# Two adds of a residual sum re-paired: the second norm's h and x2 each go into the convolution's PSUM bank

## The reference, cut to what matters

```
h = relu(layernorm(x));  x = x + L0(h)            # no edge: L0 gives 0
h = relu(layernorm(x));  x = x + agg*... + h      # layer L1; no edge: x + h
h = relu(layernorm(x))                            # layer L2: two convolutions and a residual
out = relu((h @ W1) * norm + b1)
out = (out @ W2) * norm + b2
x = x + (out + h)                                 # <- the sum that the change touches
h = relu(layernorm(x));  x = x + relu(conv(relu(conv(h))) + h)   # layer L3
```

## Time and profile before

| | |
|---|---|
| time, median of 3 runs | 3132.97 us (3106.86 to 3156.36) |
| span of the profiled execution | 2548.9 us |
| own time of the profiled execution | not listed apart; at the median, 584.1 us would lie outside its span |
| TensorE busy | 1809.8 us, 71% |
| VectorE busy | 1878.0 us, 74% |
| ScalarE busy | 1299.9 us, 51% |
| GpSimd busy | 1856.4 us, 73% |
| granted TensorE clock, mean | 0.874 of full |

### The profile page before, as it was taken

One profiled execution on the slowest core, in us unless ns is written; L12 is line 12 of the kernel. 1 busy time (PEld: TensorE's weight loads), 2 busy tenths in 40 slices (PEclk: granted clock), 3 DMA queues, 4 the chain that ended last, 5 costly groups with the idle time before them and its releaser, 6 DMA issues.

```text
span 2548.9 us, 26059 instructions
## 1 busy us (share of the span) xinstructions
PE 1809.8 (71%) x6414; PEld 875.1 (34%) x6414; DVE 1878.0 (74%) x3056; ACT 1299.9 (51%) x2694; POOL 1856.4 (73%) x1775
## 2 busy tenths in 40 slices
PE   3788877774996488878888887768888888860000
PEld 1433333322453243333444343433444344430000
DVE  7999987646888378987999788887999799960000
ACT  2767666532886264545666555545666566620000
POOL 5777777766777777756777577756777677777776
PEclk9999998886998699979999889889999899975555
DMA  2344433224776254443344356563434354440000
GB/s 65 102 125 127 118 109 84 68 72 130 232 241 220 82 167 134 134 129 105 118 125 126 106 163 194 175 190 111 123 120 126 114 145 130 133 133 23 22 22 20
DMA packets 240170, 309.75 MB, mean 122 GB/s; under 512 B 86875, under 2 KB 102389, under 8 KB 239896
## 3 DMA queue, kind: packets, MB, share of 16 engines
q1 hardware_dynamic: 183576, 281.76, 34.5%
q0 software_dynamic: 56448, 26.34, 5.8%
HBM read 188.24 MB, written 144.91 MB: 131 GB/s over the span
## 4 chain that ended last, share of the span: by engine, by line
POOL 20%; DVE 19%; PE 17%; issue 12%; ACT 6%; DMA 1%; DVEq 0%; SPq 0%; ACTq 0%; POOLq 0%
POOL mn_ring L515 12%; POOL out_dram L1883 8%; PE bank L1185 5%; DVE mn_total L1567 4%; DVE node_h L1391 4%; PE bank L1189 3%; PE bank L1194 3%; PE bank L1928 2%; PE bank L1179 2%; PE bank L1199 2%; DVE node_h L1436 1%; DVE mn_scaled L1583 1%; ACT node_square L1312 1%; ACT node_std L1296 1%; DVE node_x L1415 1%
## 5 line engine op out<-in xcount | busy, mean ns | idle before, releaser
L515 POOL DMA_INDIRECT mn_ring<-slot_rows,addr_i x980 | 1036.8, 1058 | 398.0 <-issue 293.7
L1185 PE MATMUL bank<-node_x,center 128*128 128x512 f32 x492 | 257.5, 638 | 73.0 <-DVE node_h L1391 68.9
L515 POOL DMA_INDIRECT found<-node_table,look_i x196 | 212.1, 1082 | 86.4 <-issue 63.8
L1194 PE MATMUL bank<-node_h,wconv 128*128 128x512 f32 x492 | 266.4, 625 | 0.3 <-DVE mn_sums L1701 0.3
L1189 PE MATMUL bank<-node_square,mean 128*128 128x512 f32 x492 | 259.7, 610 | 2.7 <-ACT node_std L1291 2.0
L515 POOL DMA_INDIRECT xin<-in_x_dram,src_i x196 | 205.5, 1048 | 71.7 <-issue 59.4
L1312 ACT ACTIVATE node_square<-bank 128x512 f32<-128x512 f32 x246 | 145.7, 592 | 216.1 <-PE bank L1185 215.9
L515 POOL DMA_INDIRECT xin<-in_x_dram,dst_i x196 | 206.8, 1055 | 63.5 <-issue 59.5
L1306 ACT ACTIVATE node_act<-bank,bias 128x512 f32<-128x512 f32 x246 | 168.3, 684 | 160.0 <-PE bank L1194 159.7
L1883 POOL DMA_INDIRECT out_dram<-keep,scat_i x196 | 193.0, 985 | 62.4 <-issue 62.4
L1199 PE MATMUL bank<-node_act,wconv 128*128 128x512 f32 x442 | 230.2, 603 | 2.5 <-ACT node_act L1306 2.5
(11 more groups left out here) (334 smaller groups left out, 3821.8 us busy)
## 6 DMA issues: line engine op xcount, KB each, us to landing
mn_ring<-local SPq DMA_DIRECT2D x120, 256.0 KB, 4.4
out_dram<-node_rows SPq DMA_DIRECT2D x98, 256.0 KB
mn_rin<-res SPq DMA_DIRECT2D x96, 256.0 KB, 3.7
local<-node_rows SPq DMA_DIRECT2D x96, 256.0 KB
slot_rows<-keep SPq DMA_DIRECT2D x96, 256.0 KB, 2.0
mn_fcol<-f_rows SPq DMA_DIRECT2D x192, 128.0 KB
res<-mn_x SPq DMA_DIRECT2D x72, 256.0 KB, 2.7
node_x_in<-in_x_dram SPq DMA_DIRECT2D x64, 256.0 KB, 2.9
```

Of the source, the lines that this page charges most:

```text
L515: return eng.indirect_dma_start(out=dest, out_offset=None, in_=table, in_offset=bass.IndirectOffsetOnAxis(ap=index, axis=0), bounds_check= ...
L1185: pe.matmul(bank[i][:, :], C["center"][:, :], src, start=True, stop=True).then_inc(s["centered"][i], 1)
L1194: pe.matmul(bank[5 if i == 2 else 1][:, :], C["wconv"][:, 2 * i - 4, :], nd.h[i][:, u % 2, :], start=True, stop=True) \
```

## The change

The sum of x2 and h in SBUF goes. In its place x2 is added to bank 5 together with the bias, in the bank (one SCALAR_TENSOR_TENSOR), and then h is added as the bank's result is written to x3 (one TENSOR_TENSOR). Both stand where x3 stood, after the wait for `conv2(2)`. The sums come in another order, (conv + bias + x2) + h. The buffer `res` is gone and `x2` has three slots, since it is now read one tick later. The number of instructions is the same on every engine.

```diff
-        self.x_in, self.x2, self.res, self.x3 = sb("x_in", 3), sb("x2", 2), sb("res", 2), sb("x3", 3)
+        self.x_in, self.x2, self.x3 = sb("x_in", 3), sb("x2", 3), sb("x3", 3)
...
-            center(2, nd.x2[:, (t - 1) % 2, :], s["x2"], t - 1)
+            center(2, nd.x2[:, (t - 1) % 3, :], s["x2"], t - 1)
...
-            need(act, s["res"], u - 1)
-            act.activation(nd.x2[:, u % 2, :], bank[0][:, :], ACT.Copy).then_inc(s["x2"], 1)
+            need(act, s["res"], u - 2)
+            act.activation(nd.x2[:, u % 3, :], bank[0][:, :], ACT.Copy).then_inc(s["x2"], 1)
...
         if 0 <= t - 2 < n:
             u = t - 2
-            h = normalise(2, u)
-            v.wait_ge(s["h"][2], u + 1)
-            v.wait_ge(s["x2"], u + 1)
-            v.tensor_tensor(nd.res[:, u % 2, :], nd.x2[:, u % 2, :], h, ALU.add).then_inc(s["res"], 1)
+            normalise(2, u)
         if 0 <= t - 3 < n:
             u = t - 3
             v.wait_ge(s["conv2"][2], u + 1)
+            v.wait_ge(s["x2"], u + 1)
+            v.scalar_tensor_tensor(bank[5][:, :], bank[5][:, :], C["bias"][:, 1:2], nd.x2[:, u % 3, :],
+                                   ALU.add, ALU.add).then_inc(s["res"], 1)
             v.wait_ge(s["res"], u + 1)
+            v.wait_ge(s["h"][2], u + 1)
             need(v, s["centered"][3], u - 2)
-            v.scalar_tensor_tensor(nd.x3[:, u % 3, :], bank[5][:, :], C["bias"][:, 1:2], nd.res[:, u % 2, :],
-                                   ALU.add, ALU.add).then_inc(s["x3"], 1)
+            v.tensor_tensor(nd.x3[:, u % 3, :], bank[5][:, :], nd.h[2][:, u % 2, :], ALU.add).then_inc(s["x3"], 1)
```

More of the change, by code:

```diff
@@ L1391, in normalise @@
         v.scalar_tensor_tensor(h, bank[i][:, :], 0.0, nd.std[:, i - 2, :], ALU.max, ALU.mult).then_inc(s["h"][i], 1)
-        return h
     def head(t):
```

## The result

In the measurement that belongs to the prediction the changed kernel takes 3116.55 us (median of 6, 3077.13 to 3131.16), the kernel before 3131.24 us (median of 6, 3106.86 to 3156.36), a ratio of 0.990 with a 95% interval of 0.986 to 0.994. This ratio leaves out runs more than 1.5% above their own kernel's fastest, among them the changed kernel's two longest of six; over all runs the medians stand at 0.995 and the means (3112.6 and 3132.5) at 0.994, so the gain is nearer to half a per cent. I had forecast 3180 us (3146 to 3214). The change stayed within 2%, but it went the other way and left the range.

What follows compares the result with a forecast made beforehand. The prediction took a ring of waits between VectorE and TensorE as the bound. Its terms 29.8 + 8.8 + 1.4 + 6.7 = 46.7 us, added to the measured 3132.97 us, gave 3180 us, range 3146 to 3214.

Steps and rivals of the forecast that it cites:

- A with its last ticks: Stage A: 17 ticks at 0.52 us, 8.8 us more, and 2 ticks at its end at 0.71, 1.4 us more.
- D: Stage D: the chain rests on the gathers, so nothing changes as long as they stay the longer side.
- F: Stage F: 12 ticks at 0.44 us and 2 at 0.71, 6.7 us more.
- C and E: Stages C and E: 21 ticks each at 0.71 us, 29.8 us more; the tick goes from 11.25 to 11.96 us.
- the two ticks at their ends: Ends of stages B, C, D and E: cost covered by waiting for the next stage's first gathers; without cover 5.7 us.
- Work: VectorE's instructions: 10 ns less per unit for 123 units, 1.2 us, counted as nothing.
- Rival 1: VectorE's new idle time in the ring is slack, so the delay is absorbed: 3133 us, within 8; chance 0.12.
- Rival 2: Stage D's gathers get shorter without L1409's contention, 0.048 us each, 9.4 us at most; 3124 us with slack; chance 0.04.
- Rival 3: TensorE loses its clock as the gap at `center` grows from 0.23 to 0.94 us; over 2% slower; chance 0.12.
- the median is 584.1 us above the span, and I take this as unchanged: Measured median against the profile's span of 2548.9 us: the difference stays, so 46.7 us is added to 3132.97 us.
- The ring: VectorE and TensorE waiting on each other each tick; `conv2(2)`'s end to h3's start grows 0.71 us, to 1.42.
- the case "within 2%": Whole kernel: measured time changes by less than 2% (63 us) either way; chance 0.77.

Runs made afterwards that it cites:

- e1_null: The kernel before, unedited, run against itself: 2544.41 us, ratio 1.0002.
- e4_null: The kernel before, unedited, run against itself once more: ratio 0.9994.
- e1_again: The changed kernel, unedited, measured again against the kernel before: 2592.24 us, ratio 1.0195.
- e4_again: The changed kernel, unedited, measured a third time against the kernel before: ratio 1.0199.
- e1_pos: The changed kernel's buffers, but x2 and h summed in SBUF, behind the wait for `conv2(2)`: 2592.07 us, ratio 1.0202 to the kernel before.
- e2: Both kernels with TensorE made late in every tick: the changed one took 1.8 us more with the lateness behind `conv2(2)`, 93.4 us more with it ahead.
- e5_again: The changed kernel, unedited, measured once more against the kernel before: 3122.21 us, ratio 0.9937.
- e3_bias_early: The kernel before with the bias moved into the SBUF sum ahead of the wait for `conv2(2)`: 3141.34 us, ratio 1.002 to the kernel before.
- e5_bias_early: Repeat of e3_bias_early, the kernel before with the bias in the sum ahead of the wait: ratio 0.9997 to the kernel before.
- e3_one_add: The changed kernel without the add of h, so x3 lacks this term: 3134.06 us, ratio 0.9991 to the kernel before.
- e5_one_add: Repeat of e3_one_add, the changed kernel without the add of h: ratio 1.0001 to the kernel before.
- e1_early: The changed kernel's buffers, but x2 and h summed in SBUF, ahead of the wait for `conv2(2)`: 2546.65 us, ratio 1.0016 to the kernel before.
- e2_behind_b: The kernel before with the node input's four transposes done seven times instead of once per tick, behind `conv2(2)`: 2712.98 us.

## Why the prediction was right in its steps and wrong in its number

**The steps.** Times between the first scans of the stages (for F, to the first scatter), mean of two free profiles each (e1_null and e4_null, e1_again and e4_again), against the terms of the sum:

| | before | changed | difference | forecast |
|---|---|---|---|---|
| A with its last ticks | 273.8 | 285.4 | +11.6 | 8.8 + 1.4 |
| B | 285.3 | 285.9 | +0.6 | 0 |
| C | 290.5 | 308.0 | +17.5 | 14.9 |
| D | 282.4 | 278.2 | -4.3 | 0 |
| E | 289.4 | 308.2 | +18.8 | 14.9 |
| F | 250.3 | 257.7 | +7.4 | 6.7 |

The sum is 51.6 us against 46.7. That it comes so near is in part luck: C and E are 6.5 us above their terms together, and D, at which I had put nothing, gives 4.3 back. C and E include the two ticks at their ends, of which I had said that the next stage's gathers cover them. Counted between the first gathers of the stages instead, C costs 14.7 us and D gives back 1.2, so in C the cover held; E costs 17.1, as much as all its 23 ticks at 0.74, so there it did not. The step was 0.74 per tick, not 0.71, since L1410 takes 756 ns (748 expected), L1415 691 (682 expected), and the pair stands 0.80 us apart.

- *Work:* nothing, as said. VectorE's busy time is 1880.2 us in e1_again against 1878.0. Reading the bank cost no more in these rows: the TENSOR_TENSOR at L1415, which reads it, took 691 ns in e1_again, the one in SBUF (L1409) 692 before.
- *Rival 1* (absorbed) is false in the free measurements: idle time and ticks grew together. In the paused ones the tick without a pause grew as well, and yet the time did not.
- *Rival 2* (shorter gathers) is false in the free measurements. Stage D did get shorter, which I had named as its sign, but not by its gathers: they took 1038 ns on the mean before, 1039 in e1_again, and 1036 in e1_pos, which has the SBUF sum, and the two changed kernels take the same time. In C and E the gathers did get shorter (1074 to 1021 and 1084 to 1033 ns), but in e1_pos as well (1028 and 1033), so L1409's operands aren't the reason, and the time did not follow. The rival's 0.048 us per gather is the difference of two rows (0.99 and 1.038 us); that VectorE's instructions cause it, no run shows.
- *Rival 3* (the clock) is false: the granted clock was 0.877 in e1_again, 0.874 in e1_null, and 1.00 in the steady ticks of C, where the gap at `center` had grown to 0.97 us and its four matmuls took 1.95 us. Four of them took 3.75 us in D, and the clock from 1480 to 1486 us of that profile was 0.50 of full; but that a longer gap at `center` brings such a fall, no run shows, so the chance of 0.12, and its part in the 0.20 for slower, were my estimate. The paused runs show means of 0.80 to 0.82 for both kernels alike.

**The step that failed** is the one on the numbers: "the median is 584.1 us above the span, and I take this as unchanged". Nothing of that size lies around the span: a run's time is its span and 1.8 us in the free measurements, and its span and 1.8 to 12 us in the paused ones. The changed kernel's two paused spans (3115.1 and 3100.2 us) are 523 and 508 us longer than its free ones (2591.7 on the mean), so the time lies inside the executions, most of it as pauses, of a kind that the profile that was read did not have at all. A difference of 584 us between span and time was the warning that profile and runs were of different executions, and I treated it as an additive constant. The ring's 46.7 us, right for a free execution (49.4 measured), were then added to a time in which they don't appear: it fell by 14.7 us. So the case "within 2%" came true, but not in the way forecast, and that is luck. With made pauses of TensorE in the ring, e2 shows that 49 us can be anything from 2 to 93, depending on where the lateness falls; a gain it doesn't show.

**What the pauses do to this change.** Ticks between the starts of x3's first instruction, counted in the timelines of paused profiles; "free" counts the ticks that are at most 0.15 us above the tick without a pause, the other number is the excess over it, as the mean of all ticks (A against 10.37 us for the changed kernel, 9.83 for the others):

| profile | tick of C without a pause | C, 20 ticks: free, excess, sum | A, 16 ticks: free, excess |
|---|---|---|---|
| changed, first | 11.99 | 9, 1.51, 270.1 | 16, 0.00 |
| changed, e5_again | 11.99 | 12, 1.03, 260.4 | 13, 2.05 |
| e3_bias_early | 11.19 | 8, 2.27, 269.2 | 2, 3.88 |
| e5_bias_early | 11.19 | 5, 2.12, 266.1 | 4, 4.32 |
| e3_one_add | 11.25 | 8, 2.43, 273.6 | 4, 3.16 |
| e5_one_add | 11.25 | 7, 1.96, 264.2 | 1, 2.38 |

The kernels with the short tick lose more to pauses per tick, those with the long one less, and the sums of 20 ticks overlap. In C the 0.74 us that the ring adds are met by a smaller excess. It is not VectorE's work that decides: e3_one_add has the least of it and the short tick, and is paused like e3_bias_early. Two profiles against four, each of one execution, bear this out as a pattern; they don't prove it. The two profiles of the same changed kernel differ by 33 us over 16 ticks of A, more than the gain; no paused profile of the kernel before exists, so e3_bias_early stands in for it; and no paused run varied the place alone (the kernel of e1_pos, which would, ran only in free measurements). Why a longer tick is paused less, and why enough less to end about 0.5% ahead, if that holds, stays open.

So does the origin of the pauses. Some facts narrow it. They fill idle time in the phases ahead of the node program too, which the change leaves alone (the first scan of stage A starts at 825.4 us in the first profile after, at 602.4 in e1_again), and not in the last, in which GpSimd scatters alone (264.2 and 264.6 us). Transfers don't take longer: the page's share of the queue q1, 28.3% of 3115.1 and 33.8% of 2593.8 us, comes to 882 and 877 us. And the paused traces lack records, 22,492 updates of semaphores in e5_again against 56,542 in e1_null. Every run on record has a recorded span, so whether the recording that loses these records also makes the pauses was not tested.

## What to carry to other kernels

An instruction's place against the wait that closes a ring can count for more than its length: in this kernel the same add (e1_early, e1_pos) leaves the tick of C at 11.25 us ahead of the wait and costs its full spacing, 0.73 us per tick, behind it. Before summing, check that the profiled execution's time is the time that was measured; if they differ by more than the spread of the runs, the sum holds for the profile alone, and the range must take in the executions that it doesn't show. The same change cost 2% in two free measurements and seemed to gain about 0.5% in two paused ones, so a change of 1 to 2% wants more than one measurement, each with a check of which kind it is.

## What the runs showed of the hardware that was not expected

- The same program took 2542 to 2544 us in three measurements and 3131 to 3135 us in three others (medians), with ranges of 10 and 58 us (2537.21 to 2547.52, 3103.62 to 3161.84), on chips whose numbers overlap. The changed kernel's profiles show the difference: VectorE, ScalarE and GpSimd are busy for the same time to 1%, TensorE 7% longer at a lower mean clock (0.812 against 0.877), and in the tick shown VectorE went on 2.7 us behind the row that it waits for.
- GpSimd went on gathering through such pauses: in the first profile after, from 2197.26 to 2203.03 us, its indirect DMAs start 1.30 us apart while TensorE, VectorE and ScalarE have no row at all.
- In a free measurement 24 more transposes per tick, 2.8 us of TensorE's time (346.7 us over 123 ticks in e2_behind_b), cost 2.15 us per tick behind `conv2(2)`, and took away the whole cost of an add that is no shorter for it.
